# Recurrence stage: mixes, feeds and turns in 64x64 TensorE tiles, issued in pieces at other steps

## The reference

```
ms = mean(tokens**2);  x = tokens * rsqrt(ms + 1e-4) * norm_w      # x: [16, 512, 16 heads, 16]
a_t = tanh(a)                                                      # per head 64 x 64
def step(state, x_t):                                              # 512 steps, one after the other
    state = tanh(state @ a_t + x_t @ b)                            # per head 64 states, b: 16 x 64
    mixed = state @ c + skip * x_t                                 # c: 64 x 16
    return state, mixed
out = tokens + outs @ w_out.T + b_out
```

## Time and profile before

| | |
|---|---|
| median of 3 runs (lowest, highest) | 2248.2 us (2247.14, 2248.89) |
| the profiled execution's own time | 2250.94 us |
| its span | 2249.2 us |
| PE busy | 2192.8 us (97%), 36480 matmuls |
| DVE, ACT, POOL busy | 1708.7, 1061.6, 1195.4 us |
| granted TensorE clock, mean | 0.991 |
| load of a token tile (r_x), issue to landing | 2.0 us |
| shares of the chain that ended last | PE 92%, DVE 4%, issue 1%, ACT 1% |
| recurrence: first and last matmul of `recur` | 1530.4 and 2051.5 us |

### The profile page before, as it was taken

How to read it: one execution, slowest core, us unless ns; L and a number is a source line. 1 busy time by engine, 2 the same in 40 slices (tenths; PEclk the granted TensorE clock), 3 DMA queues, 4 the chain that set the end, 5 groups by cost and what they waited for, 6 DMA issues and landing times.

```text
span 2249.2 us, 90212 instructions
## 1 busy us (share of the span) xinstructions
PE 2192.8 (97%) x36480; PEld 1535.0 (68%) x36480; DVE 1708.7 (76%) x4852; ACT 1061.6 (47%) x2707; POOL 1195.4 (53%) x1680
## 2 busy tenths in 40 slices
PE   9999999999999999999999999998999999999997
PEld 5566565556555555556777777777888888886775
DVE  5788888888887777769999999994555555555997
ACT  4655665656666665552222222222444444443444
POOL 4555555655655555536666666664444444442334
PEclk9999999999999999999999999998999999999999
DMA  4111111211211111111211011100011111111232
GB/s 150 58 50 56 67 63 62 67 58 58 67 67 58 67 59 57 56 46 31 68 33 33 30 33 33 40 24 29 28 33 37 33 33 33 37 49 37 89 94 76
DMA packets 101633, 117.81 MB, mean 52 GB/s; under 512 B 10672, under 2 KB 80080, under 8 KB 101456
## 3 DMA queue, kind: packets, MB, share of 16 engines
q1 hardware_dynamic: 101456, 115.44, 15.8%
HBM read 48.29 MB, written 33.55 MB: 36 GB/s over the span
## 4 chain that ended last, share of the span: by engine, by line
PE 92%; DVE 4%; issue 1%; ACT 1%; POOL 0%; DMA 0%; DVEq 0%; ACTq 0%; SPq 0%; POOLq 0%
PE ps_state L1731 10%; PE ps_down L1373 7%; PE ps_gate L1366 7%; PE ps_up L1366 7%; PE ps_near L812 6%; PE ps_far L592 5%; PE ps_near L584 5%; PE ps_far L584 4%; PE ps_near L592 3%; PE ps_far L627 3%; PE ps_far L611 3%; PE ps_far L604 3%; PE ps_state L1762 3%; PE ps_state L1734 2%; PE ps_r L2136 2%; PE ps_v L2147 2%
## 5 line engine op out<-in xcount | busy, mean ns | idle before, releaser
L1613 ACT ACTIVATE r_state<-ps_state 128x64 f32<-128x64 f32 x1024 | 229.4, 224 | 291.5 <-PE ps_state L1734 286.6
L1731 PE MATMUL ps_state<-r_state,later_pairs_a 64*64 64x32 f32 x8192 | 334.9, 219 | 19.7 <-ACT r_state L1613 12.5
L1731 PEld LDWEIGHTS ps_state<-r_state,later_pairs_a 64*64 64x64 f32 x8192 | 295.2, 135 | 80.2 <-issue 60.4
L1734 PE MATMUL ps_state<-r_state,later_pairs_a 64*64 64x32 f32 x8192 | 335.7, 220 | 1.9 <-issue 1.7
L480 DVE CUSTOM_DVE_ANT_0 ps_near<-ps_near,mask 128x512 f32<-128x512 f32 (+1 forms) x512 | 270.6, 590 | 84.3 <-PE ps_near L584 84.3
L340 POOL TENSOR_SCALAR_AFFINE_SELECT probsT<-probsT 128x512 f32<-128x512 f32 x256 | 160.4, 639 | 267.3 <-ACT probsT L460 167.9
L1734 PEld LDWEIGHTS ps_state<-r_state,later_pairs_a 64*64 64x64 f32 x8192 | 289.4, 135 | 2.4 <-issue 2.4
L480 DVE CUSTOM_DVE_ANT_0 ps_far<-ps_far,mask 128x384 f32<-128x384 f32 (+1 forms) x512 | 198.4, 459 | 33.6 <-PE ps_far L584 32.5
L1256 POOL TENSOR_TENSOR f_fp<-f_rounded,f_scale 128x960 f32<-128x960 f32 (+2 forms) x67 | 117.4, 1752 | 162.1 <-DVE f_rounded L1345 162.1
L1278 ACT ACTIVATE f_silu<-ps_gate 128x704 f32<-128x704 f32 x64 | 48.6, 759 | 285.7 <-PE ps_gate L1366 285.7
L592 PE MATMUL ps_far<-Q,K 32*128 32x256 f32 (+2 forms) x1536 | 182.0, 419 | 1.2 <-ACT probsT L457 0.5
(11 more groups left out here) (216 smaller groups left out, 5388.0 us busy)
## 6 DMA issues: line engine op xcount, KB each, us to landing
q_swap<-q_sin SPq DMA_DIRECT2D x128, 128.0 KB, 2.1
k_swap<-k_sin SPq DMA_DIRECT2D x128, 128.0 KB, 2.1
xT<-in_xT_dram SPq DMA_DIRECT2D x16, 512.0 KB, 3.6
xtok<-in_x_dram SPq DMA_DIRECT2D x16, 512.0 KB, 3.8
x_rows<-x SPq DMA_DIRECT2D x16, 512.0 KB, 2.9
f_x<-x_rows SPq DMA_DIRECT2D x64, 128.0 KB, 2.1
x_rows<-f_x SPq DMA_DIRECT2D x64, 128.0 KB, 1.8
r_x<-x_rows SPq DMA_DIRECT2D x64, 128.0 KB, 2.0
```

The costliest lines, as they stand in the source:

```text
L1613: nc.scalar.activation(state[:, j % 2, banks, :, t, 0, :], sums[j % 2][:, banks, :, now], ACT.Tanh).then_inc(state_ready[t], 1)
L1731: nc.tensor.matmul(sums[j % 2][half(v), stays, c, now], A[half(v), 3 * q, c, :], last[half(v), stays, c, :], start=False, stop=True, skip_ ...
L1734: out = nc.tensor.matmul(sums[j % 2][half(1 - v), changes, c, now], A[half(v), 3 * q + 1 + was, c, :], last[half(v), changes, c, :], start ...
```

## The change

The mixes, the feeds and the turn are now written as matmuls of 64x64 array tiles with operands of 64 partitions, so that all of a loop tile's matmuls have one tile shape. The weights of b and c are laid out with zeros to fill 64 rows or 64 columns.

- `mix` comes in four pieces at slots 0 to 3: per chunk a piece for the stays heads (4 matmuls of 128 columns) and one for the changes heads (8 matmuls of 64 columns). Row halves go to two different banks (MIX[c][0] and MIX[c][1]), so DVE adds twice per chunk: `scalar_tensor_tensor`, drain, `tensor_tensor`.
- `project` at slots 5 and 6.
- `turn` at slot 8: 8 ordinary matmuls against a 64x64 identity in place of 2 transposes, into two banks; it now also waits for `outs_ready`. `turned` on DVE takes four instructions of 128x64.
- the feeds in four pieces at slots 11 to 14 (stays chunk 0, stays chunk 1, changes chunk 0, changes chunk 1); the first waits for `xT_ready`, the third for `z_added`.
- At slot 0 PE waits for `inputs_in` before `recur`.

```diff
-    TURN, MIX, OUT = 1, (1, 3), (2, 0)
+    MIX, OUT, TURN = ((1, 3), (0, 2)), (1, 3), (0, 2)
...
             for c in range(CC):
-                out = nc.vector.tensor_scalar(xT[:, (j + 1) % 2, c, :], room[at][:, bank, c * P:(c + 1) * P], norm_w[:, c:c + 1], None, ALU.mult)
+                for r in range(2):
+                    bank, columns = (FIRST_TURN, slice(c * P + r * STATE, c * P + (r + 1) * STATE)) if isinstance(i, int) and i == -1 else (TURN[r], half(c))
+                    out = nc.vector.tensor_scalar(xT[:, (j + 1) % 2, c, half(r)], room[at][:, bank, columns], norm_w[:, c:c + 1], None, ALU.mult)
...
-                    nc.vector.scalar_tensor_tensor(outs[:, s, c, :], xT[:, s, c, :], skip[:, c:c + 1], room[s][:, MIX[c], 0:P],
-                                                   ALU.mult, ALU.add).then_inc(outs_ready, 1)
+                    nc.vector.scalar_tensor_tensor(outs[:, s, c, :], xT[:, s, c, :], skip[:, c:c + 1], room[s][:, MIX[c][0], 0:P],
+                                                   ALU.mult, ALU.add)
+                    dve.drain()
+                    nc.vector.tensor_tensor(outs[:, s, c, :], outs[:, s, c, :], room[s][:, MIX[c][1], 0:P], ALU.add).then_inc(outs_ready, 1)
...
+        def inputs(j, piece):
+            s, c, odd = (j + 1) % 2, piece % CC, piece // CC
+            for parity in range(1 + odd):
                 for v in range(2):
+                    for r in range(2):
+                        bank, weights_of, xT_now = 2 * r + odd, B[half(r), odd, 2 * c + v, :], xT[half(r), s, c, :]
+                        if odd:
+                            out = nc.tensor.matmul(steps_of(sums[s][half(v ^ parity), bank, c, :], parity), weights_of, steps_of(xT_now, parity),
                                                    start=(c == 0 and parity == 0), stop=False, skip_group_check=True)
+                        else:
+                            out = nc.tensor.matmul(sums[s][half(v), bank, c, :], weights_of, xT_now,
+                                                   start=(c == 0), stop=False, skip_group_check=True)
...
+        def mix(j, piece):
+            s, c, changes = (j - 1) % 2, piece // 2, piece % 2
+            for n in (1, 2) if changes else (0,):
+                for cols in range(2):
+                    for r in range(2):
+                        into = room[s][half(cols), MIX[c][r], 0:P]
+                        weights_of = C[half(r), 3 * cols + n, c, :]
+                        if n == 0:
+                            out = nc.tensor.matmul(into, weights_of, state[half(r), s, 2 * cols, c, :, 0, :], start=True, stop=False, skip_group_check=True)
+                        else:
+                            out = nc.tensor.matmul(steps_of(into, n - 1), weights_of, state[half(r), s, 2 * cols + 1, c, n - 1::2, 0, :],
+                                                   start=False, stop=True, skip_group_check=True)
+            if changes:
+                out.then_inc(mix_full, 1)
...
-        MIXES, PROJECTS, TURNS, FEEDS = (1, 3), (5, 9), 7, (13, 15)
+        MIXES, PROJECTS, TURNS, FEEDS = (0, 1, 2, 3), (5, 6), 8, (11, 12, 13, 14)
...
+                for v in range(2):
+                    for r in range(2):
+                        channels = xn[half(r), at, c * P + v * STATE:c * P + (v + 1) * STATE]
+                        out = nc.tensor.matmul(room[at][half(v), TURN[r], half(c)], channels, ident[half(r), half(r)], start=True, stop=True, skip_group_check=True)
...
                     if exists(i, 0):
+                        if at == 0:
+                            await_count(inputs_in, this_tile)
                         recur(j, t, q, states)
...
+                    if at == turns and exists(i, 1):
                         await_count(xn_ready, next_tile)
+                        if first:
+                            pe.wait_ge(*fed[1])
+                        await_count(outs_ready, states[1])
+                        turn(j)
...
+                    if at in feeds and exists(i, 1):
+                        piece = feeds.index(at)
+                        if piece == 0:
                             await_count(xT_ready, next_tile)
+                        if piece == CC:
                             await_count(z_added, this_tile)
+                        out = inputs(j, piece)
+                        if piece == 2 * CC - 1:
                             out.then_inc(inputs_in, 1)
```

More of the change, by code:

```diff
@@ L1771, in fill @@
                 nc.tensor.matmul(room[(j + 1) % 2][:, bank, :], quiet[:, 0:P], quiet[:], start=start, stop=True, skip_group_check=True)
[L1773 to L1779, removed]
-                        out = nc.tensor.matmul(steps_of(into, parity), C[:, 3 * (bank // 2) + 1 + parity, c, :], state[:, s, bank, c, parity::2, 0, :],
-                                               start=(parity == 0), stop=True, skip_group_check=True)
-                    elif parity == 0:
-                        nc.tensor.matmul(into, C[:, 3 * (bank // 2), c, :], state[:, s, bank, c, :, 0, :], start=True, stop=True)
-            return out
@@ L1788, in tensor, with first_turn @@
+        MIXES, PROJECTS, TURNS, FEEDS = (0, 1, 2, 3), (5, 6), 8, (11, 12, 13, 14)
+        FIRST_TURNS, FIRST_FEEDS = 8, (11, 12, 13, 14)
         LAST_PROJECTS, MIXING = (5, 7), 11
[L1790 removed]
+        def first_turn():
             for c in range(CC):
[L1793 removed]
+                out = nc.tensor.transpose(room[1][:, FIRST_TURN, c * P:(c + 1) * P], xn[:, 0, c * P:(c + 1) * P], ident[:])
+            out.then_inc(x_turned, 1)
@@ L1794, in turn @@
+        def turn(j):
+            at = (j + 1) % 2
+            for c in range(CC):
+                for v in range(2):
+                    for r in range(2):
+                        channels = xn[half(r), at, c * P + v * STATE:c * P + (v + 1) * STATE]
+                        out = nc.tensor.matmul(room[at][half(v), TURN[r], half(c)], channels, ident[half(r), half(r)], start=True, stop=True, skip_group_check=True)
             out.then_inc(x_turned, 1)
@@ L1842, in tensor @@
         pe.wait_ge(xn_ready, 1)
-        turn(-1, 1, MIX[1])
+        first_turn()
         def first_inputs():
@@ L1848, in first_inputs @@
             pe.wait_ge(*fed[0])
-            for c in range(CC):
-                out = inputs(-1, c)
+            for piece in range(2 * CC):
+                out = inputs(-1, piece)
             out.then_inc(inputs_in, 1)
@@ L1882, in recurrence_arrays @@
         at = (h * HEAD_DIM) % P
-        pairs_b[at:at + HEAD_DIM, 2 * chunk + v, :] = b[h]
         side, changes = bank // 2, bank % 2
+        pairs_b[at:at + HEAD_DIM, changes, 2 * chunk + v, :] = b[h]
         for order in range(1 + changes):
@@ L1888, in recurrence_arrays @@
             pairs_a[rows, 3 * side + changes + order, chunk, :] = a[h]
-            pairs_c[rows, 3 * side + changes + order, chunk, v * HEAD_DIM:(v + 1) * HEAD_DIM] = c[h]
+            column = (2 * changes + v) * HEAD_DIM
+            pairs_c[rows, 3 * side + changes + order, chunk, column:column + HEAD_DIM] = c[h]
     columns = np.concatenate([f("norm_w").reshape(CC, P).T, f("skip").reshape(CC, P).T], 1)
```

39 lines of the change are left out of this document (9 added, 30 removed).

## The result

The changed kernel took 2349.6 us, the median of 4 runs (2361.0, 2362.1, 2338.1, 2320.6), against 2248.6 before in the same series: 101 us or 4.5% more. The two longer executions lie over 1.5% above the shortest and are left out of the comparison as slow; the other two alone give a ratio of 1.035, 95% interval 1.032 to 1.038. The forecast was 2281, the range 2238 to 2312: the sign was right, the size 68 us short at the median (48 against the mean of the two shorter executions), and all four executions lie outside the range. The profiled execution took 2361.0 us (span 2359.3).

A forecast was written before the change was run, and what follows sets the result against it. PE (92% of the chain) was taken to bound it, with side pieces delaying the recurrence's second side: +0.02, +0.06 and +0.46 make +0.54 us a tile, 33 us over 62 tiles, 2284, stated as 2281; range 2238 to 2312.

The forecast's parts named there:

- rival (3): PE's loop no longer fits its code store; a 2 us fetch in each of 31 rounds, 62 us more: 2343; chance 0.03.
- Steps 1 to 3: Recurrence steps with mix pieces and projections: 2.88 us a tile against 2.82 before, +0.06.
- Steps 4 to 6 by DVE's chain: From step 4 to step 7, the third feed waits for z on DVE: 3.26 us, +0.46 a tile.
- bare step 5 of 1.08: Step 5 by PE alone: side 1 not before 0.63, the feed in slot 11 behind it, 1.08 us.
- Two signs named for "right": Step 6 longest but 7 and 0, PE idle ahead of the changes feeds; steps 0, 1 and 3 no longer than before.
- Steps 7 and 0: Around the tile's end, feed and mix pieces delay side 1: 2.17 us on average against 2.145, +0.02 a tile.
- One wait's latency, 0.14, for the new waits: At slot 0, for `inputs_in` and the mix's wait: 0.14 us added, bounds 0 and 0.28.
- the walk without waits: The step-by-step sum for steps 7 and 0 if no added wait costs anything: 2.03 us.
- DVE's added pass on `outs`: A drain and an addition per mix chunk, some 0.37 us twice, hidden ahead of projection 1 with 0.26 cover.
- Rivals (1): The sides lag but DVE is hidden; PE's sum of 7.77 us a tile, no change, 2248; chance 0.16.
- (2): The sides' lag costs nothing and z comes in time: 7.29 us a tile, -30 us, 2218; chance 0.13.
- Rival (4): The stage after the filler matmuls stays at the lower clock, costing hundreds of us; chance 0.02.

The follow-up runs named there:

- e7: The changed kernel with the turn behind slot 7 instead of slot 8, nothing else: 2318.8 us (2294.1 to 2408.5).
- e1_head0: The changed kernel with PE's inner loop aligned to begin at the start of a block of 256: 2315.0 us.
- e6: The changed kernel with side pieces behind odd slots, the old two-transpose turn, no doubled mix waits, inner loop at a block's start: 2252.0 us.
- e20: e9_base with the outer loop's head at slot 180 of a block instead of 0: 2294.4 us.
- e16: e9_base with the turn behind slot 7 instead of slot 8: 2274.2 us.
- e4: The changed kernel with DVE's two z additions moved ahead of the turned and normalise passes: 2374.9, 2310.2, 2608.1 and 2611.8 us.
- e9_base: The changed kernel with PE's outer loop aligned to begin at slot 0 of a block of 256: 2293.5 us, 1.0198 times before.
- e13: e9_base with the wait on `inputs_in` ahead of slot 0 made twice: 2302.4 us.
- e15: e9_base without the wait on side 0's last state ahead of the first mix piece: 2285.2 us.
- e1b_head230: The changed kernel with PE's inner loop begun at slot 230 of a block: 2339.3, 2317.6, 2342.0 and 7342.2 us.
- e18: The changed kernel with side pieces behind odd slots, neither doubled mix wait, its own turn, outer head at slot 0: 2235.3 us, 0.9926 times before.
- e3_odd: The changed kernel with all side pieces behind odd slots of a step (turn at slot 7): 2283.8 us (2259.1 to 2288.3).
- e2: The kernel before, its loop stretched by unused slots jumped over in mid-body and begun at slot 100: 2555.5 us, 1.135 times before.
- e21_before_jump: The kernel before with its outer head at slot 0 and a jump of a few unused slots in mid-body: 2255.1 us, 1.0016 times before.

## Why the prediction was wrong, point by point

- **The step that failed is rival (3), put at a chance of 0.03 and so at nothing in the sum.** The loop's code did not stay, and that costs 56 us of the 68 missing at the median (2349.6 less 2293.5). Its condition was met in a form that I had not looked for. I counted instructions, 1380 matrix instructions plus 152, and held them against a room of 2048; what told for the inner loop is the number of blocks that it lies in, which depends on its first slot. Its price was wrong too: not 2 us in each of 31 rounds, but some 22 us in a few: (2361.0 - 2293.5) / 3 = 22.5, for e7 (2408.5 - 2274.2) / 6 = 22.4, for e1_head0 21.5; 16.9 for e6. The 2 us of a token tile's load was the nearest row, but a round waits for nine blocks in turn, with stops of 1 to 5 us, and the granted clock falls in it as well. The product, 62 us for 31 rounds, came near by luck. The Trainium skill, Runtime: NRT & Kernel Launch, Instruction fetch mechanics, gives PE 2048 instructions in blocks of 256, filled in sequence. The trace agrees on the blocks (16.4 KB a packet, stops 256 apart), and eight blocks in use plus the next one fetched ahead would be nine in a room of eight; that is an inference, and it tells neither why e20's outer pass was spared nor why most passes of the loops in eight blocks were. Whether "some 1600 still fit" hangs on the head's slot: 1595 instructions from slot 2 were never fetched again, the same from slot 221 were.
- **Steps 1 to 3**: 2.88 forecast, 2.88 measured (0.92, 1.06, 0.90).
- **Steps 4 to 6 by DVE's chain**: 3.26 forecast, 3.20 measured; and the mechanism is shown by e16 and e4. Inside it two terms were off against each other: DVE began 0.92 behind the step's start, not 0.805 (the pause with the turn's two register waits is 0.17 and not 0.10, the turn lasts 0.46, DVE starts 0.06 behind it), and z was there 1.91 behind that, not 2.08 (`normalise` follows the last `xT` pass by 0.19, not 0.26, and the first addition follows `normalise` by 0.26, not 0.34). The forecast's bare step 5 of 1.08 is 1.28, held by `xT` (which the walk had not followed to the first feed), and step 6 is 1.05; only their sum was told. Two signs named for "right" failed with it: step 6 is not the longest of the middle steps, and step 0 is longer than before.
- **Steps 7 and 0** were the mis-sized term: 2.17 forecast, 2.43 measured in the changed kernel, 2.36 in e9_base. "One wait's latency, 0.14, for the new waits": there are three waits, the one ahead of slot 0 and two ahead of the mix, and one of them more or less is 0.15 (e13, e15). Of e9_base's 2.36 the walk without waits has 2.03, so the three come to 0.33 where 0.14 was forecast; that the rest of three times 0.15 is hidden was not tested. With one of them gone the tile is 8.30 us, which meets the forecast's length by luck, since two waits are left where it allowed for one. The other 0.06 of the changed kernel's goes with the code's place: e9 and e20 (8.44 and 8.43) do not have it, e1b_head230 (8.50) has.
- **DVE's added pass on `outs`** was hidden, as forecast: steps 1 to 3 show nothing of it.
- **Rivals (1) and (2)** fell; but (2) tells what the idea is worth if the sides do not lag: 7.29 a tile there, 7.44 in e18, which avoids the lag by its slots. Between e9 and e18 lies 1.0 us a tile: 0.84 by the slots (e3_odd has 7.60), the rest with the two waits.
- **Rival (4)** did not happen in this kernel but for its fetched rounds; e2 shows that its size, hundreds of us, can be met.

## What to carry to other kernels

Where code is added to a hardware loop, count its instructions and the slot of its head, and see how many blocks of 256 it lies in, those of an outer loop's pass too; in the trace look for packets of the instruction queue. Aligning the outer head cost nothing here and gave 56 us at the median. Where two interleaved chains share an in-order engine, put side work behind the second, and size it by where the lag goes, not by its own time. A register wait on PE cost 0.15 us here though long met: drop those that an earlier wait of the same pass already covers.

## What I had not expected

A loop can stay at the lower clock for 768 us with PE busy 99.9% (e2_before_long, 304 us lost), in a kernel whose instructions, executed at the upper level, hold that level. The jump added to it is ruled out (e21_before_jump); the fetched round at its start is the difference left, though two other kernels came out of such a round at the upper level. And one execution of e1b_head230 took 7342 us at a granted clock of 1.00; no trace shows why.
